# An adaLN block with mixture of experts: the router's one-hot rows in scalar steps on VectorE, its bias loaded earlier, its first gathers issued earlier

## The reference

```python
x = L0_attn_x                                     # 8 x 512 x 256, fp32
mod = (silu(c) @ wmod).reshape(8, 6, 1, 256)      # sa, ca, ga, sb, cb, gb
h = layernorm(x) * (1 + ca) + sa
x = x + ga * attention(h)                         # 16 heads, relative bias
h = layernorm(x) * (1 + cb) + sb
# mixture of experts: E = 8, K = 2, I = 1024
weights = softmax(h @ gate_w.T + expert_bias)
top_w, top_i = top_k(weights, 2)
top_w = top_w / (sum(top_w) + 1e-6)
out = sum over e of sparse_w[..., e] * (gelu(h @ w_up[e].T) @ w_down[e].T)
x = x + gb * (layernorm_without_affine(out) + h)
```

## Time and profile before

| | us |
|---|---|
| median of 3 runs | 1291.9 |
| the profiled execution, its own time | 1292.79 |
| its span, first to last instruction | 1291.0 |
| one-hot rows: VectorE's first (L1434) to the last matmul (L1493) | 769.18 to 795.98 |
| first `up` begins | 809.25 |

### The profile page before, as it was taken

How to read it: one execution, slowest core, us unless ns; L and a number is a source line. 1 busy time by engine, 2 the same in 40 slices (tenths; PEclk the granted TensorE clock), 3 DMA queues, 4 the chain that set the end, 5 groups by cost and what they waited for, 6 DMA issues and landing times. The chain is left out here.

```text
span 1291.0 us, 30710 instructions
## 1 busy us (share of the span) xinstructions
PE 1098.4 (85%) x11290; PEld 879.2 (68%) x11291; DVE 785.0 (61%) x2056; ACT 641.2 (50%) x913; POOL 858.3 (66%) x951
## 2 busy tenths in 40 slices
PE   5469999999999999999999503999999999999900
PEld 3237777777777777777777402888888888888800
DVE  4536667567685676856768276554555555455567
ACT  3438777776767767677677202222222222222222
POOL 2347588685976868768666428566666666767656
PEclk9779999999999999999999855999999999999955
DMA  8976753855548555485350380134424344342364
GB/s 293 275 207 188 206 166 77 205 140 112 168 100 204 134 110 162 114 196 136 90 161 11 114 299 24 39 81 83 110 45 110 48 111 114 74 85 45 45 162 134
DMA packets 122892, 167.14 MB, mean 129 GB/s; under 512 B 13048, under 2 KB 99320, under 8 KB 122784
## 3 DMA queue, kind: packets, MB, share of 16 engines
q1 hardware_dynamic: 103200, 137.59, 38.6%
q0 software_dynamic: 19584, 28.11, 11.9%
HBM read 105.22 MB, written 60.44 MB: 128 GB/s over the span
## 5 line engine op out<-in xcount | busy, mean ns | idle before, releaser
L932 DVE CUSTOM_DVE_ANT_0 b_sn<-b_ps_s,s_tile 128x512 f32<-128x512 f32 x512 | 341.3, 688 | 191.7 <-PE b_ps_s L1061 188.6
L874 ACT ACTIVATE b_pt<-b_ps_t 128x1024 f32<-128x1024 f32 x256 | 259.5, 1018 | 73.3 <-PE b_ps_t L1075 73.3
L1075 PE MATMUL b_ps_t<-s_ident,b_sn 128*128 128x128 f32 x2048 | 267.7, 273 | 3.0 <-POOL b_sn L774 1.2
L1075 PEld LDWEIGHTS b_ps_t<-s_ident,b_sn 128*128 128x128 f32 x2048 | 236.6, 141 | 40.7 <-issue 10.4
L1661 ACT ACTIVATE d_g<-d_ps_u 128x512 f32<-128x512 f32 x156 | 92.8, 598 | 314.9 <-PE d_ps_u L1774 308.3
L774 POOL TENSOR_SCALAR b_sn<-b_sn,b_mn 128x512 f32<-128x512 f32 x256 | 175.2, 695 | 101.2 <-DVE b_mn L932 100.8
L866 ACT ACTIVATE b_sn<-b_sn,b_mn 128x512 f32<-128x512 f32 x256 | 182.0, 722 | 92.4 <-DVE b_mn L932 85.4
L1061 PE MATMUL b_ps_s<-s_ks,s_qs 96*128 96x512 bf16 x512 | 179.1, 386 | 28.1 <-PEq L144 18.0
L1774 PE MATMUL d_ps_u<-d_xp,k_wu 128*128 128x256 bf16 x1776 | 201.8, 274 | 0.0
L1789 PE MATMUL d_ps_y<-k_wd,d_gp 128*128 128x256 bf16 x1776 | 199.9, 273 | 0.0
L1774 PEld LDWEIGHTS d_ps_u<-d_xp,k_wu 128*128 128x128 bf16 x1776 | 173.7, 98 | 21.6
(11 more groups left out here) (199 smaller groups left out, 1191.5 us busy)
## 6 DMA issues: line engine op xcount, KB each, us to landing
w_parts<-b_w_split SPq DMA_DIRECT2D x32, 512.0 KB, 3.6
splits<-s_parts SPq DMA_DIRECT2D x32, 384.0 KB, 2.9
s_qs<-splits SPq DMA_DIRECT2D x96, 128.0 KB, 5.9
s_ks<-splits SPq DMA_DIRECT2D x96, 128.0 KB, 7.4
b_w_raw<-in_w_up_t SPq DMA_DIRECT2D x16, 512.0 KB, 10.8
b_w_raw<-in_w_down_t SPq DMA_DIRECT2D x16, 512.0 KB, 7.1
k_wu<-w_parts SPq DMA_DIRECT2D x8, 1024.0 KB
k_wd<-w_parts SPq DMA_DIRECT2D x8, 1024.0 KB
```

Source lines behind the costliest of these rows:

```text
L874: act.activation(pt[:, m, 2 * pair:2 * pair + 2, :], ps_t[:, 2 * pair:2 * pair + 2, :], ACT.Exp).then_inc(exped, 1)
L932: dve.tensor_tensor_reduce(sn[:, n % 2, t, :], ps_s[:, t % 2, :], ahead.tile[:, n, at:at + S], -1.0, BIG, ALU.add, ALU.min, mn[:, n % 2, t ...
L1075: mm = pe.transpose(ps_t[:, j, t * P:(t + 1) * P], sn[:, m, t, j * P:(j + 1) * P], ident[:, :])
```

## The change

- `e_bias` is allocated at the top and loaded in `prepare` among the constants (`load_weights`), third in SyncE's list there; one wait of `prepare` (L363) goes from 32 to 48. The load and the wait in `route` go.
- `route`: VectorE makes a bf16 copy of `iota_p`, `iota_b`, once. For each of the 64 groups it then issues three `tensor_scalar`: `hot_rest` (equal to a per-partition value), and `hot_fill` twice (equal to a per-partition value, times the constant i; equal to a per-partition value, times the per-partition `place`). In and out are bf16. GpSimd's and ScalarE's shares and the `placed` signal go. TensorE waits for 3 instructions per group. The tables L1443 to L1456 still follow on VectorE.
- `xg` and `x_in` move to `Kept`. GpSimd waits in `route` for `kept.tokens` and there issues the four indirect DMAs of tiles 0 and 1, with `kept.tokens` as the offsets and no copy. Their two `load`s in `experts` go.
- The identity of `prepare` is kept and used in `experts`; the second one goes.

```diff
+        engine.dma_start(self.e_bias[:, :], expert_bias.rearrange("(a e) -> a e", a=1).to_broadcast([P, NE])).then_inc(self.const_in, 16)
...
-                dve.wait_ge(ahead.const_in, 32)
+                dve.wait_ge(ahead.const_in, 48)
...
-            sp.dma_start(e_bias[:, :], expert_bias.rearrange("(a e) -> a e", a=1).to_broadcast([P, NE])).then_inc(e_bias_in, 16)
...
-            pool.wait_ge(placed, 1)
-            pool.wait_ge(consts_ready, 7)
-            for i in range(2 * NT - BY_POOL, 2 * NT):
-                pool.tensor_scalar(hot_rest[:, i, :], iota_p, place_f[:, 1, i:i + 1], None, ALU.is_equal).then_inc(rest_done, 1)
+            pool.wait_ge(tokens_set, 1)
+            for u in range(2):
+                for i in range(TT):
+                    pool.indirect_dma_start(kept.xg[:, u, i, :], None, h2_rows,
+                                            bass.IndirectOffsetOnAxis(ap=kept.tokens[:, u * TT + i:u * TT + i + 1], axis=0)
+                                            ).then_inc(kept.x_in[u], 16)
...
-            act.wait_ge(consts_ready, 7)
-            for i in range(0, 2 * NT, AT_ONCE):
-                ...
-                act.activation(fill_by[:, 1, at, :], hot_fill[:, at, :], ACT.Copy, scale=place[:, :]).then_inc(fill_act, 1)
...
-            dve.wait_ge(e_bias_in, 16)
...
+            dve.tensor_copy(iota_b[:, :], iota_p)
...
-            dve.sem_inc(placed, 1)
-            for i in range(0, 2 * NT, AT_ONCE):
-                ... (hot_rest L1434, hot_fill L1436, fill_by L1439, 8 groups each)
+            for i in range(2 * NT):
+                dve.tensor_scalar(hot_rest[:, i, :], iota_b[:, :], place_f[:, 1, i:i + 1], None, ALU.is_equal).then_inc(hot_rows, 1)
+                dve.tensor_scalar(hot_fill[:, i, 0, :], iota_b[:, 0:FILLS], place_f[:, 0, i:i + 1], float(i),
+                                  ALU.is_equal, ALU.mult).then_inc(hot_rows, 1)
+                dve.tensor_scalar(hot_fill[:, i, 1, :], iota_b[:, 0:FILLS], place_f[:, 0, i:i + 1], place[:, :],
+                                  ALU.is_equal, ALU.mult).then_inc(hot_rows, 1)
...
-            dve.tensor_scalar(kept.tokens[:, :], source[:, 1, :], -1.0, 0.0, ALU.add, ALU.max)
+            dve.tensor_scalar(kept.tokens[:, :], source[:, 1, :], -1.0, 0.0, ALU.add, ALU.max).then_inc(tokens_set, 1)
...
+                pe.wait_ge(hot_rows, 3 * i + 3)
+                mm = pe.matmul(ps_f[:, 0:2 * FILLS], hot_rest[:, i, :], hot_fill[:, i, :, :].rearrange("p s f -> p (s f)"),
+                               start=(i == 0), stop=(i == 2 * NT - 1))
...
-            make_identity(pool, ident, zeroed, ident_ready)
-            for u in range(2):
-                load(u, u)
```

More of the change, by code:

```diff
@@ L59, with __init__ @@
 class Ahead:
-    def __init__(self, nc, ctx):
+    def __init__(self, nc, ctx, ident, e_bias):
+        self.ident, self.e_bias = ident, e_bias
         self.tile = ctx.enter_context(nc.sbuf_tensor("s_tile", [P, NH, ZW], F32))
@@ L139, with prepare @@
 FOR_NEXT = ("q0", "k0", "q1", "k1", "v0", "v1")
-def prepare(nc, ahead, x, c_t, wmod, rel_rev, w_qkv, b_qkv, w_out, b_out, gate_t, mod_rows, ext_rows, splits, h1t):
+def prepare(nc, ahead, x, c_t, wmod, rel_rev, w_qkv, b_qkv, w_out, b_out, gate_t, expert_bias, mod_rows, ext_rows, splits, h1t):
     with ExitStack() as ctx:
@@ L212, in _ @@
             ahead.load(sp, ext_rows, 0)
-            ahead.load_weights(sp, w_qkv, b_qkv, w_out, b_out, gate_t)
+            ahead.load_weights(sp, w_qkv, b_qkv, w_out, b_out, gate_t, expert_bias)
             for k in range(2):
@@ L1239, in __init__, with route @@
         self.filled = sb("filled", [P, NE], I32)
+        self.xg = sb("xg", [P, 2, TT, D])
+        self.x_in = [ctx.enter_context(nc.semaphore(f"k_x_in{slot}")) for slot in range(2)]
         self.wu = sb("wu", [P, 2, PIECES, DC, NI], BF16)
         self.wd = sb("wd", [P, 2, PIECES, NIC, D], BF16)
-def route(nc, kept, logits, rest_rows, mod_rows, expert_bias, w_parts, gate_rows):
+def route(nc, kept, logits, rest_rows, mod_rows, e_bias, w_parts, gate_rows, h2_rows):
     FILLS = TABLE * TT
-    BY_POOL = 3 * NT // 4
-    AT_ONCE = 8
     with ExitStack() as ctx:
@@ L1293, in route @@
         hot_rest = sb("hot_rest", [P, 2 * NT, P], BF16)
-        hot_fill = sb("hot_fill", [P, 2 * NT, FILLS], BF16)
-        fill_by = sb("fill_by", [P, 2, 2 * NT, FILLS], BF16)
+        hot_fill = sb("hot_fill", [P, 2 * NT, 2, FILLS], BF16)
+        iota_b = sb("iota_b", [P, P], BF16)
         found = sb("found", [P, 2, FILLS])
@@ L1486, in _, with experts @@
             for i in range(2 * NT):
[L1487 to L1493, removed]
+                pe.wait_ge(hot_rows, 3 * i + 3)
+                mm = pe.matmul(ps_f[:, 0:2 * FILLS], hot_rest[:, i, :], hot_fill[:, i, :, :].rearrange("p s f -> p (s f)"),
+                               start=(i == 0), stop=(i == 2 * NT - 1))
             mm.then_inc(tokens_found, 1)
-def experts(nc, kept, w_parts, h2_rows, gate_rows, sums, out):
+def experts(nc, kept, ident, w_parts, h2_rows, gate_rows, sums, out):
     BANKS = 4
@@ L1513, in experts @@
         gates = sb("gates", [P, 2, TT])
-        xg = sb("xg", [P, 2, TT, D])
+        xg, x_in = kept.xg, kept.x_in
         xp = sb("xp", [P, 2, PIECES, DC * ROWS], BF16)
@@ L1832, in adaln_block @@
         logits = ctx.enter_context(nc.sbuf_tensor("logits", [P, NT, NE], F32))
+        ident = ctx.enter_context(nc.sbuf_tensor("ident", [P, P], F32))
+        e_bias = ctx.enter_context(nc.sbuf_tensor("e_bias", [P, NE], F32))
         with ExitStack() as ctx_ahead:
-            ahead = Ahead(nc, ctx_ahead)
-            prepare(nc, ahead, x, c_t, wmod, rel_rev, w_qkv, b_qkv, w_out, b_out, gate_t, mod_rows, ext_rows, splits, h1t)
+            ahead = Ahead(nc, ctx_ahead, ident, e_bias)
+            prepare(nc, ahead, x, c_t, wmod, rel_rev, w_qkv, b_qkv, w_out, b_out, gate_t, expert_bias, mod_rows, ext_rows, splits, h1t)
             attention(nc, ahead, logits, x, h1t, mod_rows, ext_rows, splits,
@@ L1838, in adaln_block @@
         kept = Kept(nc, ctx)
-        route(nc, kept, logits, rest_rows, mod_rows, expert_bias, w_parts, gate_rows)
-        experts(nc, kept, w_parts, h2_rows, gate_rows, sums, out)
+        route(nc, kept, logits, rest_rows, mod_rows, e_bias, w_parts, gate_rows, h2_rows)
+        experts(nc, kept, ident, w_parts, h2_rows, gate_rows, sums, out)
 def kernel(**inputs):
```

30 lines of the change are left out of this document (5 added, 25 removed).

## The result

| | before | after |
|---|---|---|
| median, 9 runs each on one chip | 1291.9 us | 1298.35 us |
| the profiled execution, its own time | 1292.79 | 1299.91 |
| its span | 1291.0 | 1298.1 |
| first `up` begins | 809.25 | 817.99 |

The ratio after to before is 1.0049, with a 95% interval of 1.0037 to 1.0061: 6.4 us slower. The prediction said slower and 1295.9. The sign and the main term came out. The hand-off to the experts gave back 2 us less than forecast.

The account below looks back on a forecast made before the run. Bound: the router's chain on VectorE up to the first `up`, then TensorE. Front -2.6 - 0.1 + 0.2, rows and tables +32.5 + 4.1 - 26.84, hand-off -3.4: +3.9, rounded to +4.0, so 1295.9 us; range 1286 to 1302.

Parts of the forecast that it names:

- The bias: Start of route: VectorE's 2.66 us wait for the bias goes, and about 2.6 us come back whole.
- the extra issue in `prepare`: SyncE's added bias load issue, about 0.5 us, costed at nothing because VectorE's split holds a later store.
- Start of the rows: Before the one-hot rows in route: signal to GpSimd removed, -0.1 us; bf16 copy of 128 numbers added, +0.2.
- The 192 scalar steps: One-hot rows on VectorE in route: 0.508 us a group, 32.5 us for 64 groups, replacing 26.8 us on three engines.
- the price of an operand: In VectorE's scalar steps: one per-partition operand adds 0.057 us, two add 0.11, taken in full.
- The tables: L1443 to L1456 on VectorE, between the last scalar step and L1459: lose their cover and cost 4.1 us whole.
- Tokens to first `up`: Hand-off from router to experts: 11.9 us becomes 8.5 through earlier gathers, the copies and the identity, -3.4.
- The first tiles: First `up` on TensorE at the low clock: its 1.8 us loss moves along, may differ by up to 1.8; nothing added.
- cheap steps: Rival on the scalar steps: a queue hides the per-partition operand's cost; 18.2 us at four a tick, 1281.5; chance 0.17.
- two operands as one: Rival on the scalar steps: two operands fetched as one, 0.455 us a group, 29.1 us, 1292.4; chance 0.10.
- two elements a tick: Rival on the scalar steps: 37.6 us, +9.0, 1300.9; chance 0.13.
- The end of the block: Rival on route's end: it waits for GpSimd's gathers to land, not just their issue; +5.6, 1297.5; chance 0.10.

Follow-up runs that it names:

- e1_steps_only: Kernel before plus the scalar steps on VectorE and the kept identity, with bias load and gathers where they were before; 1299.4 us, ratio 1.0058 to before.
- e4_more_operands: Changed kernel with one more per-partition operand in each of the first two of a group's three steps; 1310.27 us, one run.
- e5_fp32_in: Changed kernel with fp32 numbers in place of their bf16 copy as input of all three steps, outputs still bf16; 1300.32 us, one run.
- e2_no_steps: Changed kernel without its scalar steps: one-hot rows on VectorE, GpSimd and ScalarE as before; 1288.3 us, ratio 0.9971 to before.
- e3_tables_late: Changed kernel with the table steps moved behind the places, to the end of VectorE's program in the block; 1297.9 us, ratio 1.0042 to before.
- e8_one_tile: Changed kernel with only tile 0's two gathers in the router's block, tile 1's back in the experts' block; 1305.91 us, one run.
- e9_wide_late: As e6_wide, with the tables moved behind the places; 1280.6 us, ratio 0.9916 to before.
- e7_packed_late: As e9_wide_late, but with 8 groups innermost, VectorE's tensor_tensor operands bf16 at unit step, and the product by i on VectorE; 1284.34 us, ratio 0.9940 to before.
- e6_wide: Changed kernel with one-hot rows by VectorE tensor_tensor, 8 groups at once, both products on ScalarE, none on GpSimd; 1280.5 us, ratio 0.9913 to before.

## Why the prediction was right, and where it was off

It forecast slower, 1295.9; measured is 1298.35. Point by point:

- **The bias**, -2.6: the wait for it is gone and the distance shrank by 2.6. Right. That the extra issue in `prepare` costs nothing was not tried by itself. The attention block's first matmul came at 75.4 (before) and 73.9 us (`e1_steps_only`) without it, and at 71.5 to 76.4 in the ten profiles with it: half a microsecond would not show there.
- **Start of the rows**, -0.1 and +0.2: both right within 0.1.
- **The 192 scalar steps**, 32.5 us: 33.6. The mechanism held in each part: the price of an operand (0.057 forecast, 0.060 in `e4_more_operands`), and four elements a tick (`e5_fp32_in`). The size was 3% low: the third step, with two operands, takes 0.21 instead of 0.20, the other two 0.314 together instead of 0.308. Over 64 groups that is +1.1 us.
- **The tables**, 4.1 us without cover: 3.6, with no idle time before `found`. This is the "some tenths faster with GpSimd quiet" that the prediction named and did not take: from the first to the last of these steps it is 3.9 us beside GpSimd's rows (before and `e2_no_steps`) and 3.5 in after. `e3_tables_late` shows that they lie on the path.
- **Tokens to first `up`**, -3.4: only -1.4. This is the term that was mis-sized. The prediction put the block's end 0.27 us after the last engine's last instruction, read from a block that ended on VectorE, and carried it over to one that ends on a gather. In its place the block waits until the rows have landed (`e8_one_tile`): 3.2 us lie between the start of the last gather and the next block's first instruction (811.83 to 815.07), where the prediction had 1.3. That is +1.9. GpSimd issued the first gather 0.3 us after the tokens' end, not 0.8, now without a copy of its own ahead of it: -0.5. With all rows landed, turn(0), turn(1) and `up` stand one behind the other and take 2.9 us from the block's start, where 2.5 was forecast: +0.4. The rest is rounding.
- **The first tiles**: 0.7 us were gained where nothing was added. The prediction had allowed for this, by up to 1.8 either way. The granted clock before the first `up` is always at 0.50, the lower of the two levels (1.2 GHz), and goes to 1.00 (2.4 GHz) during it: 2.2 us after its start in after, 3.7 in before. In the profiles here the first `up` took from 6.5 to 7.6 us by that.
- **Sum**: +1.1 (steps), -0.5 (tables) and +2.0 (hand-off) on the forecast of +3.9 give +6.5; measured +6.4. So the forecast is 2.5 us low as a sum of one error of +2.0 and two that partly cancel.

The rivals: cheap steps are ruled out (`e4_more_operands`), and so are two operands as one (the third step costs the full second operand) and two elements a tick (`e5_fp32_in`). The end of the block is confirmed (`e8_one_tile`), and it stands beside the forecast, not against it: 1295.9 and 1.6 more is 1297.5. It should have been a term of the sum with two bounds, and not a case of 0.10.

Left open: the attention block ends between 740.6 and 749.3 us in the profiles of these kernels, which share its code. Two things move it. Its first matmul comes between 71.5 and 76.4 us, and from there to the last logits it takes 667.6 to 668.2 us in four profiles (before, `e1_steps_only`, `e2_no_steps`, `e9_wide_late`), but 672.2 to 673.0 in six. In those six TensorE's granted clock was at 0.50 for 10.2 us from 719 to 724 on, well before its fall at 730 to 737 that all twelve have. In after it was for 6.8 us (0.70 from 722 to 732, before 0.95) and the block took 670.7; in `e5_fp32_in` for 3.4 us, and it took 668.8. So an early fall costs some 4 us, on top of what the change does. Nothing tried here says what decides it. Of the ten kernels with the bias loaded in `prepare` eight had it, of the two without none, one profile each; whether the earlier load has a part in it is not shown. It may be why medians and distances part: `e1_steps_only` is +6.6 by the medians and +9.85 by the distance to the first `up`, `e7_packed_late` -7.1 and -10.1, `e9_wide_late` -10.3 and -13.4.

## What to carry over

Price a short instruction by its fixed part, one part for each per-partition operand, and only then its elements: at 82 or 128 bf16 elements the elements were 0.02 to 0.03 of 0.15 to 0.21 us, so a split into small steps loses even where each runs at the widest rate. Then compare like with like: of the gain of the wide rows on VectorE, the greater part was a product that moved to ScalarE. Before moving a transfer into an earlier block to hide it, ask whether that block's end waits for it to land: the gathers gave back 1.4 us here (with the identity) where 3.4 were forecast. And before giving an engine a layout that suits it, look at who reads the result: the packed rows won 3.7 us on VectorE (15.1 to 11.4 for 64 groups, with a product more) and cost TensorE 7.7 (11.4 to 19.1).

## What the runs showed of the chip

- A per-partition scalar operand costs VectorE 0.060 us, in a queue of independent steps too (`e4_more_operands`, 128 of them, 7.73 us); a second operation beside it added nothing.
- Behind a block that ends on GpSimd's gathers, the next one began 0.72 to 0.80 us after their last bytes (ten profiles; after and `e8_one_tile` differ in the number of gathers).
- A matmul of 128 x 128 by 128 x 164 took TensorE 0.30 us with both bf16 operands at a 16-byte step, against 0.18 us when they were contiguous, both at a granted clock of 0.50 (`e7_packed_late`, `e6_wide`).
- `tensor_tensor` with all operands bf16 and unit step innermost moved 1024 elements in 0.60 us, start to start, where the fp32 form took 1.13 (`e7_packed_late`, `e6_wide`).
- ScalarE's copies of 82 elements with a constant scale follow each other at 0.16 us (`e6_wide`, eight from 770.18, the next step at 771.47).
